# Two transformer blocks on one core: the residual sums of block 1 move to GpSimd, and the attention banks are released at the scaling

## What is computed

```python
z = _mha(x, x, Wq1, Wk1, Wv1, mask0, causal=True)
x1 = _layernorm(x + z, ln1_g, ln1_b)
z = _mha(x1, context, Wq2, Wk2, Wv2, mask1, causal=False)
x2 = _layernorm(x1 + z, ln2_g, ln2_b)
z = jnp.maximum(x2 @ fc1_w.T + fc1_b, 0.0) * mask0
z = (z @ fc2_w.T + fc2_b) * mask0
x3 = _layernorm(x2 + z, ln3_g, ln3_b)
...
weights = jax.nn.softmax(qh @ kh / np.sqrt(dk) + bias + graph_attn_bias, axis=-1)
out = (weights @ vh) @ wo + bo + x3
out = layernorm(out, ln_g, ln_b)
```

## Time and profile before

| what | before |
|---|---|
| median of 3 runs (lowest to highest) | 341.50 us (341.49 to 341.51) |
| the profiled execution's own time | 341.61 us |
| its span in the trace | 339.8 us |
| mean granted TensorE clock in the span | 0.995 |
| busy in the span: PE, PEld | 320.3 us, 252.3 us |
| busy in the span: DVE, ACT, POOL | 291.3, 239.9, 241.6 us |

### The profile page before, as it was taken

The page is one execution under the profiler, slowest core; times in us unless marked ns, Lnnn a source line. Parts: engine busy times, 40 slices in busy tenths (PEclk is TensorE's granted clock), DMA queues, the critical chain, the costliest instruction groups (busy, mean ns, idle before and its releaser), DMA issues.

```text
span 339.8 us, 13231 instructions
## 1 busy us (share of the span) xinstructions
PE 320.3 (94%) x5328; PEld 252.3 (74%) x5333; DVE 291.3 (86%) x836; ACT 239.9 (71%) x567; POOL 241.6 (71%) x376
## 2 busy tenths in 40 slices
...
DMA packets 13180, 17.87 MB, mean 53 GB/s; under 512 B 1601, under 2 KB 10177, under 8 KB 13121
## 3 DMA queue, kind: packets, MB, share of 16 engines
...
HBM read 15.99 MB, written 1.05 MB: 50 GB/s over the span
## 4 chain that ended last, share of the span: by engine, by line
PE 56%; DVE 26%; ACT 5%; issue 5%; POOL 4%; DMA 1%; SPq 1%; POOLq 0%; ACTq 0%; DVEq 0%
PE C_E L632 5%; PE C_E L577 4%; PE B_E L451 3%; PE C_E L622 3%; PE A_E L432 3%; PE B_E L432 3%; PE C_E L593 2%; DVE A_mx L889 2%; PE A_E L451 2%; DVE A_S L897 2%; PE C_E L609 2%; PE B_E L465 2%; DVE Sc L973 2%; DVE C_den L991 2%; DVE L_xh L943 2%
## 5 line engine op out<-in xcount | busy, mean ns | idle before, releaser
L1025 POOL TENSOR_TENSOR A_kblk<-A_qk,cst 128x1024 f32<-128x1024 f32 x16 | 30.3, 1897 | 25.5 <-DVE A_qk L865 25.4
L1046 POOL TENSOR_TENSOR L_xg<-L_xh,vec_sb 128x128 f32<-128x128 f32 x64 | 29.2, 456 | 15.9 <-DVE L_xh L943 13.9
L1035 POOL TENSOR_TENSOR L_rstd<-L_ve,cst 128x1 f32<-128x1 f32 x64 | 35.1, 548 | 5.0
L1077 POOL TENSOR_TENSOR Sc<-Sc,C_mx 128x512 f32<-128x512 f32 x28 | 29.1, 1046 | 9.4 <-DVE C_mx L983 9.3
L763 ACT ACTIVATE qT<-C_E,bq 128x128 f32<-128x128 f32 x112 | 31.9, 379 | 4.1 <-PE C_E L577 3.9
L1033 POOL TENSOR_TENSOR L_ve<-L_mv,cst 128x1 f32<-128x1 f32 x64 | 12.1, 189 | 29.4 <-DVE L_mv L930 28.8
L1086 POOL TENSOR_TENSOR Pc<-Pc,C_rd 128x512 f32<-128x512 f32 x28 | 29.0, 1043 | 2.8 <-DVE C_rd L993 2.5
L1025 POOL TENSOR_TENSOR B_kblk<-B_qk,cst 128x1024 f32<-128x1024 f32 x16 | 30.3, 1897 | 0.0
L577 PE MATMUL C_E<-x3T,wq_sb 128*128 128x128 f32 x224 | 29.6, 279 | 0.4 <-ACT x3T L755 0.4
L577 PEld LDWEIGHTS C_E<-x3T,wq_sb 128*128 128x128 f32 x224 | 27.0, 192 | 1.1 <-ACT x3T L755 0.7
L632 PE MATMUL C_E<-wo_sb,C_zT 128*128 128x128 f32 x224 | 27.5, 276 | 0.1
...
## 6 DMA issues: line engine op xcount, KB each, us to landing
...
```

The lines of the kernel that those rows point to most:

```text
L1025: tt(a.kblk[:], a.qk[:, 1].unsqueeze(1).to_broadcast([P, 8, P]), at["rmask"].unsqueeze(2).to_broadcast([P, 8, P]), ALU.mult).then_inc(a.s_ ...
L1035: tt(l.rstd[:], l.ve[:], at["power"], ALU.pow).then_inc(l.s_rstd, 1)
L1046: tt(l.xg[:], l.xh[:], l.g, ALU.mult).then_inc(l.s_xg, 1)
L1077: tt(v, v, place(n).mx[:, 8 * g:8 * g + 8].unsqueeze(2).to_broadcast([P, 8, S]), ALU.subtract).then_inc(C.s_sub, 1)
```

## The change

The scaled result and the residual sum leave PSUM: both are one SBUF tile now, `A_zn` and `B_zn`, and the sum is made in place. The sum `y` moves from DVE to POOL. As bank X is read for the last time by `zn`, the PE steps that waited for `xh` wait for `zn` (semaphore `s_zn`, two counts a round). `xh` of L1 and L2 takes the form that L4's has. The last zero products wait for `zn` too, and are 9 steps instead of 6. PLAN is a new list of the same steps, with three `L.warm` more.

```diff
-COOL = 6
+COOL = 9
...
-            a.y, a.zn = a.X[:, 2 * P:3 * P], a.X[:, 3 * P:4 * P]
+            a.y = a.zn = sb(name + "_zn", [P, D])[:]
...
-                pe.wait_ge(L2.s_xh, PAIRS)
+                pe.wait_ge(Bc.s_zn, 2 * PAIRS)
                 idle_products(Bc.X[:, :], 3)
...
-            def energy(a, l, causal):
+            def energy(a, causal):
...
                     if n:
-                        pe.wait_ge(l.s_xh, n)
+                        pe.wait_ge(a.s_zn, 2 * n)
...
-                        pe.wait_ge(L1.s_xh, n)
+                        pe.wait_ge(A.s_zn, 2 * n)
...
-                        pe.wait_ge(L2.s_xh, n)
+                        pe.wait_ge(Bc.s_zn, 2 * n)
...
-                    pe.wait_ge(L1.s_xh, PAIRS)
+                    pe.wait_ge(A.s_zn, 2 * PAIRS)
...
-                    if l is L4:
+                    if l is not L3:
                         dve.scalar_tensor_tensor(l.xh[:], l.y, l.mv[:, 0:1], l.rstd[:].to_broadcast([P, D]),
                                                  ALU.subtract, ALU.mult).then_inc(l.s_xh, 1)
...
+            def y(a, l):
+                def step(n):
+                    pool.wait_ge(a.s_zn, 2 * n + 2)
+                    tt(l.y, a.zn, xs[:, n] if a is A else x1[n % RING][:], ALU.add).then_inc(l.s_y, 1)
+                return step
...
-C.ks_1#1 A.z#0 C.k_0#2 C.chi#4 A.zn#0 C.k_1#2 A.y#0 C.ks_0#2 A.st#0 C.ks_1#2 C.k_0#3 A.rstd#0 C.k_1#3 C.ks_0#3
...
```

More of the change, by code:

```diff
@@ L914, in zn @@
                 return step
-            def y(a, l):
-                def step(n):
-                    dve.wait_ge(a.s_zn, 2 * n + 2)
-                    tt(l.y, a.zn, xs[:, n] if a is A else x1[n % RING][:], ALU.add).then_inc(l.s_y, 1)
-                return step
             def stats(l):
@@ L1088, in nrm @@
                 return step
[L1090 removed]
+            steps = {"A.y": y(A, L1), "B.y": y(Bc, L2), "C.x3c": x3c, "C.clo": clo, "C.sub_0": c_sub(0), "C.sub_1": c_sub(1), "C.nrm_0": nrm(0), "C.nrm_1": nrm(1),
                      "A.kblk": kblk(A), "B.kblk": kblk(Bc),
@@ new lines @@
+C.vs_1#3 B.qkv#2 B.zn#1 A.y#3 C.bvo#0 B.qk#2 B.y#1 A.st#3 B.3gb#0 B.st#1 B.q0#2 A.v#4 B.rstd#1 B.e0#2
+C.obias#0 A.rstd#3 C.x3t#0 B.nz#2 B.xh#1 C.x3ts#0 B.cnt#2 A.e#4 B.v#2 B.gb#1 B.cut#2 A.xh#3 B.f1#1 B.kblk#2
+A.max_0#4 A.qkv#5 B.f1s#1 C.chi#8 A.max_1#4 B.f2#1 C.q_0#0 A.qk#5 A.sub_0#4 B.f2s#1 A.sub_1#4 A.gb#3 B.f3#1
+A.exp_0#4 B.e#2 B.y3#1 C.qs_0#0 C.clo#8 A.q0#5 B.am#3 C.q_1#0 B.max_0#2 A.exp_1#4 C.x3c#0 B.cm#3 B.3st#1
+A.pt_0#4 C.qs_1#0 B.max_1#2 A.pt_1#4 B.3rstd#1 B.sub_0#2 A.e0#5 B.sub_1#2 C.e#0 B.exp_0#2 B.3xh#1 B.exp_1#2
@@ new lines @@
+C.zt#0 A.nz#6 A.sub_0#5 A.y#4 A.sub_1#5 B.e#3 B.rstd#2 C.zts_0#0 A.st#4 C.zts_1#0 B.xh#2 A.cnt#6 B.max_0#3
+A.exp_0#5 B.gb#2 C.e#1 A.exp_1#5 A.cut#6 A.rstd#4 B.sub_0#3 B.f1#2 A.pt_0#5 B.f1s#2 C.fadd_0#1 B.exp_0#3
+A.kblk#6 B.f2#2 A.pt_1#5 C.fadd_1#1 B.f2s#2 B.pt_0#3 A.pts_0#5 B.max_1#3 C.loadf#1 B.f3#2 A.pts_1#5 C.o#0
+A.xh#4 C.loadf#0 B.sub_1#3 A.gb#4 B.y3#2 B.exp_1#3 B.pts_0#3 B.3st#2 B.pt_1#3 A.v#6 B.3rstd#2 A.pv_0#5
+B.pts_1#3 B.pv_0#3 B.am#4 A.pv_1#5 B.3xh#2 B.pv_1#3 B.cm#4 C.max_0#1 A.zts#5 A.qkv#7 B.3gb#2 B.zts#3 C.y#0
@@ new lines @@
+C.v_0#7 A.max_0#9 C.pts_1#4 B.kblk#7 B.v#7 C.v_1#7 C.vs_0#7 A.max_1#9 C.zt#4 C.vs_1#7 A.xh#8 A.sub_0#9
+C.chi#12 B.gb#6 B.e#7 A.sub_1#9 A.exp_0#9 A.gb#8 A.exp_1#9 B.f1#6 B.max_0#7 A.pt_0#9 C.zts_0#4 A.pt_1#9
+C.rstd#3 B.sub_0#7 B.f1s#6 C.zts_1#4 A.qkv#10 B.max_1#7 B.f2#6 C.clo#12 A.qk#10 C.e#5 B.exp_0#7 A.q0#10
+B.sub_1#7 A.pts_0#9 C.gb#2 B.am#8 A.e0#10 A.pts_1#9 C.xh#3 C.fadd_0#5 B.f2s#6 A.pv_0#9 B.exp_1#7 A.pv_1#9
+C.fadd_1#5 B.f3#6 A.zts#9 B.pt_0#7 B.cm#8 B.y3#6 C.loadf#5 A.z#9 B.pts_0#7 B.pt_1#7 C.store#2 B.3st#6 C.o#4
@@ new lines @@
+A.qk#11 B.f1#7 C.zt#5 C.vs_0#8 A.q0#11 A.sub_0#10 B.f1s#7 A.max_1#10 A.exp_0#10 B.f2#7 C.v_1#8 A.rstd#9
+A.sub_1#10 B.f2s#7 C.zts_0#5 B.f3#7 C.zts_1#5 A.xh#9 A.e0#11 B.y3#7 A.gb#9 A.exp_1#10 C.e#6 A.nz#11 C.vs_1#8
+B.3st#7 C.x3c#5 B.am#9 B.3rstd#7 A.cnt#11 A.pt_0#10 C.fadd_0#6 A.pt_1#10 C.gb#3 A.pts_0#10 B.3xh#7 B.e#8
+C.max_0#6 B.cm#9 A.pts_1#10 C.fadd_1#6 C.store#3 C.sub_0#6 A.pv_0#10 B.max_0#8 A.pv_1#10 C.loadf#6 B.tr#9
+C.rstd#4 B.max_1#8 C.exp_0#6 C.o#5 A.zts#10 B.sub_0#8 B.3gb#7 B.sub_1#8 B.exp_0#8 C.xh#4 B.xts#9 C.x3t#7
```

300 lines of the change are left out of this document (139 added, 161 removed).

## The result

The changed kernel took 345.48 us in the median of 4 runs (345.38 to 346.03), against 341.5 us before: 1.0109 times as long, 95% interval 1.0082 to 1.0137; the profiled execution took 345.38 us. The forecast was 338.2 us and faster; it is 4 us slower, beyond the range's 342.8 us.

A forecast was written before the change was run, and what follows sets the result against it. PE (busy 255.3 of the middle 260 us) and DVE (242.4 us) were taken to bound it by turns. The terms -2.3 - 1.4 - 0.65 + 0.6 + 0.5 = -3.25 gave 338.2 us, range 334.5 to 342.8 us.

The forecast's parts named there:

- POOL gains the sums: 32 sums of 456 ns on POOL, 14.6 us, priced at its 4% chain share: 0.6 us more, bounds 0 and 14.6.
- signs of being wrong: DVE's wait before statistics above 8 us, `xh` of L1 and L2 above 0.5 us, or chain over POOL well over 4%.
- DVE loses 8.7 us, priced at 2.3: DVE sheds sums (9.4 us), `xh` adds 1.05, statistics save 0.35; at chain share 0.26, 2.3 us less.
- rule on shared reads: DVE instructions with two SBUF inputs contend with POOL's SBUF reads, the later blocking fully; the change makes 32 more.
- rival (0.06, 341.0 us): Shared reads eat the saving: each of 32 new `xh` takes 756 ns; 341.0 us, chance 0.06.
- DVE's wait for `rstd`: DVE's 2.5 us stand before `xh` in the middle, filled by steps put between: 0.65 us less, 0 to 2.5.
- Early release: PE gets the banks at the scaling's end instead of `xh`'s: 1.4 us less, bounds 0 and 2.3 us.
- DVE waits for the sums: DVE stands 1.9 us for POOL's sums before the statistics; at DVE's chain price 0.5 us more.
- rival of late sums: Sums behind A's key blocks on POOL, DVE standing 0.6 us a round: 343.4 us, chance 0.17.
- Order: The rest of the new order of steps, most keeping their neighbours: 0, give or take 1.5 us.
- Zero products: Three more steps, 9 matmuls in the tail where PE stands anyway: costed at nothing, up to 1.2 us.

The follow-up runs named there:

- clean pair: Kernel before, old order, sum on DVE from the bank into SBUF, `xh` on ACT: bank released at the sum 348.60 us, released at `xh` 352.44 us.
- unclear one: Changed kernel's code in the old order: bank released at the scaling 369.75 us, released at `xh` 372.29 us; the intervals overlap.

## Why the prediction was wrong, point by point

*POOL gains the sums (+0.6 us):* the first step that failed, and two of the prediction's own signs of being wrong came with it: 23% of the chain over POOL, and `xh` of L1 and L2 at 0.52 us in the mean. It took POOL's share of the chain, 4%, as the price of more work on POOL, and 61 us of free time as room for it. The load alone costs 5.5 us in the kernel before. A share tells what the engine cost as things stood; 53.8 of POOL's free 61 us were waits at the head of its list for DVE, and an instruction put into an in-order list delays all behind it. The prediction looked for the price in one place, DVE's wait for the sums; it came up at POOL's other customers.

*DVE loses 8.7 us, priced at 2.3:* 3.8 us came. `xh` cost 4.1 us more over all norms instead of 1.05, by the rows' totals (24.0 + 6.5 against 7.0 + 19.4 us). The forecast took L4's mean, saying that its 16 ran among the same neighbours; the new ones of A were stretched more (560 ns against L4's 437). The rest is a matter of counting: durations of DVE's rows sum to 326.8 us where the page counts 291.3 us busy, because neighbours overlap. The rows' sum fell by 5.3 us, to 321.5 us, and the busy time by only 3.8 us. That DVE's time has a price was right: in the new order the sums on DVE cost 6.5 us.

*The rule on shared reads:* the second step that failed. It was weighed and set aside for size ("half of the 16 stayed below 349 ns"). For most of the 32 that was right: B's median is 352 ns. But the long ones reach 1895 ns, the length of one `A_kblk` or `B_kblk`, and carry the mean. The Trainium skill, SBUF — State Buffer, section Who interferes with whom, says that whoever comes later blocks fully until the other is done. The 1.12 us in the timeline above agrees, and so does the sum, 291 ns with one SBUF operand and 568 to 780 ns with two. The section also says that a `tensor_scalar` can enter a mode that contends: its 1834 ns from SBUF agree. As a rival (0.06, 341.0 us) it was priced through DVE's work alone, 1.6 us net at DVE's chain price, 0.4 us. In the old order, with sums on DVE and POOL at its old load, the run with `xh` from SBUF is 13.2 us slower than before, for 11.4 us more in `xh`. In the changed kernel `xh` takes 4.1 us more; how much of the 4 us comes from it stays open.

*DVE's wait for `rstd` (-0.65):* did not come. Over the span it was 6.1 us before (5.2 and 0.9) and is 5.2 us now (4.3 and 0.9); that the steps put in between gave time and the sums ahead of `rstd` on POOL took it back is likely, but not shown.

*Early release (-1.4, bounds 0 and 2.3):* undersized if anything, 3.8 us in the clean pair and 2.5 us in the unclear one, both with a late `xh`. What it gives in the new order could not be isolated.

*DVE waits for the sums (+0.5):* right, 2.5 us of standing against 1.9. The rival of late sums (0.17, 343.4 us) had the sign and not the mechanism: DVE would have had to stand 0.27 us a round more and stands 0.08. (In B's round 5 what stands ahead of the sum is `B_kblk`, not `A_kblk`, and in round 0 too; both take 1.9 us.) *Order (0, give or take 1.5):* no term of its own, and the margin was far too narrow; identical code moved by 24, 3 and 6 us. *Zero products (0):* not tried.

With DVE's measured saving and the measured load in their places the sum is -0.26 x 3.8 - 1.4 + 5.5 + 0.5 = +3.6 us, 345.1 us. That it meets 345.48 is luck: with 3.8 us for the release it is +1.2 us, with 6.5 us for the sums off DVE it is -1.9 us, and the terms come from different programs.

The runs also allow another path to the changed kernel, by medians: sums kept on DVE, `xh` from SBUF, old order, 355.00 us; the new order, 351.97 us; the sums to POOL with the release at the scaling, 345.48 us. On this path the loss comes in with `xh` from SBUF, and moving the sums gains 6.5 us. So it is shown that 4% of 14.6 us was a wrong price for load on POOL, and that `xh` from SBUF can cost far more than the 0.26 x 1.05 us taken for it; how the changed kernel's 4 us divide between them is not shown.
